# Gated cross-attention and experts block: another order of work inside a slot, and half of the weights' low parts on another engine

## The reference, cut to what matters

```python
x = x + tanh(g_xattn) * xattn(layernorm(x), ctx)      # 16 heads of 8, softmax, Wout
x = x + tanh(g_ffn)   * ffn(layernorm(x))
# ffn, x [8, 128, 128]:
gate = softmax(x @ Wg.T); topk_val, topk_idx = top_k(gate, 2)
comb = (one_hot(topk_idx) * (topk_val / (sum(topk_val) + 1e-9))[..., None]).sum(-2)
for e in range(8):
    a, b = split(x @ W1[e].T + b1[e], 2)               # 256 + 256
    out += ((a * sigmoid(b)) @ Wo.T + bo) * comb[..., e]
```

## Time and profile before

| | |
|---|---|
| median of 3 runs | 126.2 us (124.78, 126.2, 126.21) |
| the profiled execution, own time | 124.31 us |
| its span | 122.2 us |
| busy: PE, DVE, ACT, POOL | 111.3, 99.6, 66.1, 83.7 us |
| weights loading (PEld) | 76.7 us |
| granted TensorE clock over the span | 0.998 of full speed |

### The profile page before, as it was taken

The page is one execution under the profiler, slowest core; times in us unless marked ns, Lnnn a source line. Parts: engine busy times, 40 slices in busy tenths (PEclk is TensorE's granted clock), DMA queues, the critical chain, the costliest instruction groups (busy, mean ns, idle before and its releaser), DMA issues.

```text
span 122.2 us, 2512 instructions
## 1 busy us (share of the span) xinstructions
PE 111.3 (91%) x808; PEld 76.7 (63%) x810; DVE 99.6 (81%) x274; ACT 66.1 (54%) x145; POOL 83.7 (68%) x106
## 2 busy tenths in 40 slices
PE   6989798899699979797979999999999799999982
PEld 2254554466466646564746877878686687878661
DVE  5489999779897989898795969599999778776770
ACT  3166467849586866675768266543433334343520
POOL 6359879997989599984235587857273987574600
PEclk9999999999999999999999999999999999999999
DMA  3999970000000000000000000000000000000001
GB/s 92 325 360 414 421 303 5 0 0 8 0 3 0 0 8 0 0 5 0 0 0 0 0 5 3 0 21 0 21 5 3 21 20 2 0 24 0 21 0 43
DMA packets 3468, 6.53 MB, mean 53 GB/s; under 512 B 384, under 2 KB 2048, under 8 KB 3456
## 3 DMA queue, kind: packets, MB, share of 16 engines
q1 hardware_dynamic: 3024, 5.66, 12.8%
q10 hardware_dynamic: 432, 0.72, 1.7%
HBM read 5.85 MB, written 0.52 MB: 52 GB/s over the span
## 4 chain that ended last, share of the span: by engine, by line
PE 52%; DVE 29%; issue 11%; ACT 4%; POOL 2%; DVEq 0%; ACTq 0%; POOLq 0%
PE ps L955 11%; PE ps L957 10%; PE ps L956 10%; DVE neg_max L613 9%; DVE gl L685 3%; PE ps L974 2%; PE ps L927 2%; DVE qk_lo L600 2%; PE ps L904 2%; DVE w_lo L796 2%; DVE max_m L792 2%; PE ps L1094 2%; ACT sig L448 1%; PE ps L984 1%; DVE att L783 1%
## 5 line engine op out<-in xcount | busy, mean ns | idle before, releaser
L328 POOL TENSOR_TENSOR gacc<-gacc,gl 128x256 f32<-128x256 f32 x38 | 28.6, 753 | 12.9 <-DVE gl L685 9.4
L448 ACT ACTIVATE sig<-ps 128x512 f32<-128x512 f32 (+1 forms) x33 | 19.3, 585 | 28.3 <-PE ps L957 25.8
L685 DVE SCALAR_TENSOR_TENSOR gl<-ps,comb,sig 128x256 f32<-128x256 f32 (+1 forms) x57 | 24.6, 471 | 5.0 <-ACT sig L448 4.7
L955 PE MATMUL ps<-w_hi,x_hi 128*128 128x512 f32 x64 | 27.3, 427 | 0.0
L956 PE MATMUL ps<-w_lo,x_hi 128*128 128x512 f32 x64 | 25.3, 395 | 0.0
L957 PE MATMUL ps<-w_hi,x_lo 128*128 128x512 f32 x64 | 25.3, 395 | 0.0
L394 ACT ACTIVATE probs<-ps 128x1024 f32<-128x1024 f32 x16 | 16.4, 1024 | 7.7 <-PE ps L914 7.5
L613 DVE TENSOR_REDUCE neg_max<-ps 128x8 f32<-128x1024 f32 x16 | 19.4, 1215 | 0.7 <-PE ps L887 0.6
L955 PEld LDWEIGHTS ps<-w_hi,x_hi 128*128 128x128 f32 x64 | 12.1, 188 | 3.0 <-DVE gl L685 0.6
L957 PEld LDWEIGHTS ps<-w_hi,x_lo 128*128 128x128 f32 x64 | 12.0, 188 | 2.9
L956 PEld LDWEIGHTS ps<-w_lo,x_hi 128*128 128x128 f32 x64 | 12.1, 190 | 1.9
(11 more groups left out here) (126 smaller groups left out, 209.4 us busy)
## 6 DMA issues: line engine op xcount, KB each, us to landing
...
```

The costliest lines, as they stand in the source:

```text
L328: nc.gpsimd.tensor_tensor(gacc[:, t % 2, :], gacc[:, t % 2, :], gl[:, e - 1, :], ALU.add).then_inc(pool_experts_added, 1)
L448: nc.scalar.activation(sig[:, n % 3, e[0]:e[1], :], ps[:, b + e[0]:b + e[1], HH:H2], ACT.Sigmoid).then_inc(act_sigmoids, 1)
L685: nc.vector.scalar_tensor_tensor(dst[:, c[0]:c[1]], ps[:, 2 * (n % 3) + e % 2, c[0]:c[1]], comb[:, t, e:e + 1], sig[:, n % 3, e % 2, c[0]: ...
L955: mm(o, x_hi[:, t, :], w_hi[:, e, :], start=True, stop=False)
```

## The change

It leaves nearly all instructions as they are and places them otherwise in the slots:

- **PE.** `weighted(i-1, 1)` now stands behind the first scores of the slot, ahead of the values' projection and of Wout. The turn of `o_sb` stands ahead of the second scores, and the turn of `att` right behind them. In odd slots the turn of `xn2` moves behind the first scores. The idle matmuls of slot 1 are dropped.
- **DVE.** `rden` and `att` go between the instructions of the moments and ahead of the second maxima. `low_parts` moves to the end of even slots. The bias for the values (`bvl`) is made after the second maxima of slot 0 and not ahead of `max_m`, and `bout_t` is made in slot 1.
- **ACT.** `values_out` goes ahead of `values_in`.
- **POOL.** In even slots it makes `w_lo` of expert i, at the end of its slot, once ACT has rounded `w_hi`. DVE makes those of the odd slots alone.

The diff, cut to its core:

```diff
+                if on(i) and i % 2 == 0:
+                    pool.wait_ge(act_w1_high, i + 1)
+                    nc.gpsimd.tensor_tensor(w_lo[:, i, :], w1[:, i, :], w_hi[:, i, :].bitcast(fp32),
+                                            ALU.subtract).then_inc(pool_w1_low, 1)
...
-                if i % 2 == 1 and i != 1 and on(i + 3):
+                if i in (-3, -1):
                     xn_turned_out((i + 3) // 2)
                 if on(i):
                     exp(i, 0)
-                if i == 1:
-                    xn_turned_out(2)
+                if i % 2 == 1 and i >= 1 and on(i + 3):
+                    xn_turned_out((i + 3) // 2)
                 if i == 0:
                     high_parts(1)
+                if on(i - 1) and i < T:
+                    values_out(i - 1)
                 if i % 2 == 0 and on(i + 2):
                     values_in((i + 2) // 2)
-                if on(i - 1) and i < T:
-                    values_out(i - 1)
...
+                    "p k (h c) -> p k h c", h=2)
+
+            rd = rden[:, :].rearrange("p (k h) -> p k h", h=2)
+            sums_inverted = [0]
...
+            def inverse_sums(t):
+                dve.wait_ge(pe_values_turned, t + 1)
+                sums_inverted[0] = mark(nc.vector.reciprocal(rd, attended_heads()[:, :, :, HD]))
+
+            def attended(t):
+                if t >= 2:
+                    dve.wait_ge(pe_attended_turned, t - 1)
+                dve.wait_ge(dve_chain, sums_inverted[0])
+                nc.vector.tensor_tensor(att[:, t % 2, :].rearrange("p (k h c) -> p k h c", h=2, c=HD),
...
-                if on(i - 3):
-                    t = i - 3
-                    dve.wait_ge(act_xn2, 2 * (t + 1))
...
+                if on(i - 3) and (i % 2 == 0 or i >= T):
+                    x_low(i - 3)
                 if on(i + 1):
                     maxima(i + 1, 0)
+                if on(i - 3) and i % 2 == 1 and i < T:
+                    x_low(i - 3)
                 if i == 0:
-                    statistics(2)
-                if i % 2 == 0 and i > 0 and on(i + 2):
-                    low_parts((i + 2) // 2)
+                    late = moments(2)
+                if i == 1:
+                    dve.wait_ge(pe_value_bias, 1)
+                    nc.vector.scalar_tensor_tensor(bout_t[:, :], boutb, tanh_g[:, 0:1], ps[:, VEB, 0:D], ALU.mult,
+                                                   ALU.add).then_inc(dve_bout_scaled, 1)
                 if on(i - 2):
...
-                    link(nc.vector.bn_stats(stats2[:, t % 2, :], x1[:, t, :]))
-                    link(nc.vector.bn_aggr(mv2[:, t % 2, :], stats2[:, t % 2, :]))
+                    moments2 = mark(nc.vector.bn_stats(stats2[:, t % 2, :], x1[:, t, :]))
+                if on(i - 1) and i < T:
+                    inverse_sums(i - 1)
+                if on(i - 2):
+                    t = i - 2
+                    dve.wait_ge(dve_chain, moments2)
+                    moments2 = mark(nc.vector.bn_aggr(mv2[:, t % 2, :], stats2[:, t % 2, :]))
+                if on(i - 1) and i < T:
+                    attended(i - 1)
+                if on(i - 2):
+                    t = i - 2
+                    dve.wait_ge(dve_chain, moments2)
                     nc.vector.tensor_scalar(var2[:, t % 2:t % 2 + 1], mv2[:, t % 2, 1:2], LN_EPS, None,
                                             ALU.add).then_inc(dve_variance2, 1)
...
                 if i == 0:
-                    low_parts(1)
-                if i == -1:
-                    low_parts(0, (1,))
+                    variances(2, late)
                     dve.wait_ge(dve_ones, 1)
                     nc.vector.tensor_scalar(bvl[:, :], ones_r[:, :].bitcast(fp32), bvc, None,
                                             ALU.mult).then_inc(dve_v_bias, 1)
+                    nc.vector.tensor_tensor(wgT[:, :], wg_in, wg_last, ALU.subtract).then_inc(dve_ffn_weights, 1)
...
-                if i == 0:
...
-                    nc.vector.tensor_tensor(wgT[:, :], wg_in, wg_last, ALU.subtract).then_inc(dve_ffn_weights, 1)
...
-                if on(i - 1):
-                    t = i - 1
-                    dve.wait_ge(pe_values_turned, t + 1)
...
-                        dve.wait_ge(pe_attended_turned, t - 1)
-                    link(nc.vector.reciprocal(rd, o[:, :, :, HD]))
-                    nc.vector.tensor_tensor(att[:, t % 2, :].rearrange("p (k h c) -> p k h c", h=2, c=HD),
...
+                if i == T:
+                    inverse_sums(T - 1)
+                    attended(T - 1)
...
-                if on(i):
+                if i % 2 == 0 and i >= 0 and on(i + 2):
+                    low_parts((i + 2) // 2)
+                if on(i) and i % 2 == 1:
                     dve.wait_ge(act_w1_high, i + 1)
                     nc.vector.tensor_tensor(w_lo[:, i, :], w1[:, i, :], w_hi[:, i, :].bitcast(fp32),
                                             ALU.subtract).then_inc(dve_w1_low, 1)
...
+            def turn_values(t):
+                pe.wait_ge(act_values, t + 1)
+                if t == 0:
+                    pe.wait_ge(dve_bout_scaled, 1)
+                else:
+                    pe.wait_ge(dve_x1, t)
...
+            def turn_attended(t):
+                pe.wait_ge(dve_attended, t + 1)
+                pe.wait_ge(act_v, min((t + 1) // 2 + 2, NP))
+                if t >= 2:
+                    pe.wait_ge(act_logits, t - 1)
+                nc.tensor.transpose(ps[:, AB, 0:P], att[:, t % 2, :], ident).then_inc(pe_attended_turned, 1)
...
+            def turn_xn2(t):
+                i = t + 3
+                if i <= T + 1:
+                    pe.wait_ge(act_attended, i - 1)
+                else:
+                    pe.wait_ge(act_gated, 1)
+                pe.wait_ge(act_normed2, t + 1)
+                nc.tensor.transpose(ps[:, AB, 0:P], xn2[:, t % 2, :], ident).then_inc(pe_xn2_turned, 1)
...
-                    pe.wait_ge(dve_w1_low, 2 * j + 2)
+                    pe.wait_ge(pool_w1_low, j + 1)
+                    pe.wait_ge(dve_w1_low, j + 1)
...
-                if i % 2 == 1 and i != 1 and on(i + 3):
-                    turn_xn((i + 3) // 2)
-                if on(i - 3):
...
                 if i == -1:
+                    turn_xn(1)
                     keep_busy(FILL[3], PVB)
+                if i == -3:
+                    turn_xn(0)
+                if on(i - 3) and (i % 2 == 0 or i >= T):
+                    turn_xn2(i - 3)
                 if on(i):
                     scores(i, 0)
                 if i == 0:
                     project(1)
-                if i == 1:
-                    turn_xn(2)
+                if i % 2 == 1 and 3 <= i < T:
+                    turn_xn2(i - 3)
+                if i % 2 == 1 and i >= 1 and on(i + 3):
+                    turn_xn((i + 3) // 2)
+                if on(i - 1) and i < T:
+                    weighted(i - 1, 1)
                 if i % 2 == 0 and on(i + 2):
                     project_values((i + 2) // 2)
                 if on(i - 2):
...
-                if on(i - 1) and i < T:
-                    weighted(i - 1, 1)
+                if i == 1:
+                    pe.wait_ge(act_out_weights, 1)
+                    pe.wait_ge(dve_v_bias, 1)
+                    pe.wait_ge(dve_max_masked, 2)
+                    mm(ps[:, VEB, 0:D], bvl[:, :], wout_t[:, :], start=True, stop=True).then_inc(pe_value_bias, 1)
...
+                if on(i - 1) and i < T:
+                    turn_values(i - 1)
                 if on(i):
                     scores(i, 1)
-                if i == 0:
...
-                    mm(ps[:, VEB, 0:D], bvl[:, :], wout_t[:, :], start=True, stop=True).then_inc(pe_value_bias, 1)
-                if on(i - 1):
-                    t = i - 1
-                    pe.wait_ge(act_values, t + 1)
-                    if t == 0:
-                        pe.wait_ge(dve_max_masked, 2)
-                    else:
-                        pe.wait_ge(dve_x1, t)
...
+                if on(i - 1) and i < T:
+                    turn_attended(i - 1)
+                if i == T:
+                    turn_values(T - 1)
                 if on(i):
                     weighted(i, 0)
-                if on(i):
-                    pe.wait_ge(act_v, min(i // 2 + 2, NP))
-                    if i >= 3:
-                        pe.wait_ge(act_logits, i - 2)
-                    keep_busy(WARM[0] if i < 2 else WARM[1], AB)
+                if i == 0:
+                    pe.wait_ge(act_v, 2)
+                    keep_busy(WARM, AB)
...
-                    if t == 1:
-                        pe.wait_ge(dve_bout_scaled, 1)
-                    elif t >= 2:
+                    if t >= 2:
                         pe.wait_ge(dve_attended, t - 1)
                     nc.tensor.transpose(ps[:, VEB, 0:P], neg_max[:, t % 2, :], ident).then_inc(pe_maxima_turned, 1)
-                if on(i - 1):
-                    t = i - 1
```

(34 more changed lines are left out.)

45 lines of the change are left out of this document (13 added, 32 removed).

## The result

The changed kernel is slower: 138.6 us median of four executions (133.72, 142.42, 134.86, 142.59) against 125.5 us (124.03 to 126.21). The ratio is 1.080 [1.055, 1.104]. Each ratio in this document is made from a kernel's executions within about 1.5% of its fastest, so it leaves out most of those whose clock fell, while a median holds them all. What sets the four apart is the clock of TensorE: their spans are 131.9, 140.6, 133.1 and 140.8 us at a mean granted clock of 0.934, 0.842, 0.897 and 0.842. My forecast was 127.6 us, with a range from 124.0 to 130.3. What follows is read from the execution of 133.72 us, against the profiled 124.31 us of before (span 122.2).

A forecast was written before the change was run, and what follows sets the result against it. It took the succession of slots 0 to 7 as the bound, with POOL late after the change. Start +1.4, slots 4 and 5 +1.26, slot 6 -0.5, slot 7 -0.7, rounded to +1.4 on 126.2: 127.6 us, range 124.0 to 130.3.

The forecast's parts named there:

- the sum: 1.4 + 1.26 - 0.5 - 0.7 = +1.5 us, rounded down to +1.4, over the start, slots 4 and 5, 6, and 7.
- Part 1: Turn of the maxima on PE no longer behind `att`: gain of 0.6 us per slot, hidden because POOL is late.
- Part 2: `rden`, `att` before the second maxima: S (start of a slot's first score matmul) to `var` 4.23 us, even slots.
- Part 3: Half of `w_lo` moved to POOL: POOL pays 1.27 us each, `q_lo_m` in even slots 1.0, DVE regains 0.68 to 0.84.
- rival of a stretched POOL: POOL's `w_lo` and weights run at 1.72 us, `q_lo_m` at 1.49, as beside DVE's `w_lo`: 130.3 us; chance 0.20.
- Part 4: Chain from `var` through POOL, ACT and PE, slots 4 and 5: 13.67 us a pair against 12.41, +1.26.
- Part 5: Start: up to 1.9 us earlier, but POOL's first `w_lo` waits for `w_hi`; S(4) at 40.2, +1.4 us.
- Part 6: Slot 6, without projection, -0.5 us; slot 7, with `att` made ahead of the routing, -0.7 us.
- Part 7: Edits at nothing: `values_out` ahead of `values_in`, `wgT`, `bout_t`, turn of `xn2` behind the first scores in odd slots.
- fit in: Rival: POOL has room, slot pairs cost what they did, the rest is gain, -2.8 us: 123.4 us; chance 0.15.
- even out: Rival: two unknown handovers at 0.33, slots 4 and 5 cost nothing, S(4) 0.5 late: -0.7, 125.5 us; chance 0.20.
- chance of slower: Probability of a time above 128.7 us, 0.29: 0.18 from stretched POOL, 0.11 from the forecast's own case.

The follow-up runs named there:

- experiment 9: The changed kernel plus idle matmuls wherever its PE was seen to wait (slots 1 to 3 and 5 to 7): 128.3 us, ratio 1.027.
- experiment 11: The changed kernel with only POOL's first `w_lo` moved from slot 0 to slot 6: 124.75, 133.66, 127.42 and 133.12 us.
- experiment 8: The kernel before, with DVE's `rden` and `att` of slot 7 ahead of the routing: 125.4 us, ratio 1.007.
- number 10: The changed kernel with POOL's four `w_lo` moved to slots 6 and 7, plus six idle matmuls in slot 1: 124.7 us, ratio 1.002.
- Number 3: The changed kernel with four idle matmuls behind each turn of the maxima in slots 1 to 6: 131.4 us, ratio 1.053.

## Why the prediction was wrong

**The step that failed** is one that the sum did not have: it took PE's clock as 1.00 throughout. The last sentence of the prediction called a lower granted clock "a cost that the sum lacks". I read 1.00 in both stretches and went on, with no rival and no bound for it. It measured 6.2 us of the 9.7 (experiment 9), and more in the executions of 142 us. The danger could have been seen: the change adds waits to PE in a stage where PE already stood idle 0.89 of 10 us, and takes idle matmuls away in the same place. What the trace of before could not give is how many gaps are too many: from 30 to 32 us its PE worked 1.18 of 2 us, and its clock stayed at 1.00. Nor do the runs give it as a rule: in one and the same kernel (11) the clock held once and fell three times.

The queues were priced too low besides. With the clock held (experiment 9) they cost 3.5 us, where the sum had 1.5:

| | S(4) | S(4) to S(6) | slot 6 | S(7) to the end |
|---|---|---|---|---|
| foreseen | +1.4 | +1.26 | -0.5 | -0.7 |
| with the clock held | +2.6 | +0.9 | -0.6 | +0.6 |

By its own parts:

- **Part 1, right.** The turn of the maxima waits for nothing (54.90 above), where the earlier trace rows had 0.28 for `att`. As the prediction said, the gain does not show.
- **Part 2, right.** S to `var` was put at 4.23 us in even slots. With the clock held (experiment 9) it is 45.63 - 41.41 = 4.22 in slot 4, and no term is off by more than 0.12. Of the two handovers that no row showed, Wout (begun at 43.66) to `x1` took 0.42, where I took 0.54, and the turns (begun at 44.60) to `rden` 0.46, where I took 0.50. DVE waits 0.67 and 0.36 for them:

```profile
44.08 0.29 DVE L789 TENSOR_TENSOR x<-ps,x 128x128 f32<-128x128 f32 x1 [0.67 <-PE ps L1112]
45.06 0.26 DVE L733 RECIPROCAL rden<-ps 128x16 f32<-128x16 f32 x1 [0.36 <-PE ps L888]
...
45.63 0.14 DVE L803 TENSOR_SCALAR var<-mv 128x1 f32<-128x1 f32 x1
```

- **Part 3, right.** POOL's four `w_lo` take 1.28 us in the mean, and `q_lo_m` fell from 1.32 to 1.09. The price was read off the right row: `w` has a median of 1.27 both before and after. The lines of POOL after:

```profile
L322 POOL TENSOR_TENSOR w<-w,w1l 128x512 f32<-128x512 f32 x8 | 10.6, 1328 | 0.0
L317 POOL TENSOR_TENSOR q_lo_m<-qk_lo,pk 128x512 fp32r<-128x512 f32 x8 | 8.8, 1094 | 0.0
...
L367 POOL TENSOR_TENSOR w_lo<-w,w_hi 128x512 fp32r<-128x512 f32 x4 | 5.1, 1276 | 1.5 <-ACT w_hi L522 1.5
```

  The rival of a stretched POOL falls with this: none of the four ran at 1.72. Beside one of them (experiment 9, begun at 47.72) DVE ran both `qk_lo`, at 47.93 and 48.33, and it took 1.29 us, as the prediction expected of operands in PSUM. POOL was stretched in other places, though: its sum `x` took 2.83 us, not 2.37, beside DVE's `w_lo` of slot 1 (at 25.25), and one of the eight `w` took 1.73.
- **Part 4, right in its mechanism, somewhat high in size.** From S(4) to S(6) I put 13.67 us. It is 13.54 after, in part at a lower clock, and 13.31 with the clock held: +0.9 to +1.1 against +1.26. By its terms, with the clock held: S to `var` 4.22; from `var` to the end of the weights (50.96 + 1.28) 6.61, where I had 6.63; from there to S(6), at 54.72, 2.48, where I had 2.81. The last term is the one that is off. It also left out 0.24 us that the earlier trace rows show, ACT's wait ahead of `attT`: those rows give 51.20 - 48.15 = 3.05. In the new order `att` is turned early and that wait is gone, but I gave no such reason.
- **Part 5, right in its mechanism, short in size.** `w_lo` of slot 0 begins at 20.07 behind ACT (19.8 foreseen), `w_hi` of slot 3 at 37.98 (37.4 foreseen). S(4) was put at 40.2 and came at 42.18. Of these 2.0 us, 0.5 is POOL (the weights end at 37.94; nearly all of it is the stretched `x`). The other 1.4 lie between the weights and S(4), 4.24 us and not 2.81. With the clock held and no matmul added, the same piece takes 2.90 us (experiment 11: 36.01 to 38.91), so 1.3 of it is the clock. That 2.90 lies near my 2.81 is in part luck, as the path is another one. In the chain of the kernel after it doesn't go through `xn2` and `attT`: the turn of `att` on PE waits for `lg`, the copied logits, which come behind ACT's late `w_hi` (0.42 in the row at 38.81, and 0.44 in experiment 11), and PE's own work follows it up to S(4). POOL's delay reaches PE through more than one reader of ACT's queue. In experiment 9, S(4) is 1.2 us later than foreseen: 1.0 up to the end of the weights (38.38, not 37.4), 0.2 from there.
- **Part 6, half right.** Slot 6 took 60.04 - 54.72 = 5.32 us with the clock held, 5.36 foreseen. Slot 7's 0.7 is not there; experiment 8 shows that the routing pays for it. In experiment 9 `comb` begins 8.3 us after S(7) (68.33 - 60.04), not 5.8, and from S(7) to the end it takes 0.6 us more than before, not less.
- **Part 7**, the edits put at nothing: no run tests them one by one. The sign "expert stage of the same length" failed: from S(7) to the end it took 68.0 us, not 65.1, as the first matmuls ran at half speed up to 70 us; with the clock held it is 65.7.

**The rivals.** POOL does not fit in, nor does it even out: `w_hi` of slot 3 began at 37.98, not before 36. The chance of slower, 0.29, was too small because its cases priced only queues. Had the clock been a rival, rows of before could have bounded its price. As an estimate: ten us like those of the earlier trace rows hold 9.11 us of PE's work, which at half the clock would fill 18.2 us, so a long fall in this stage costs several us.

**What stays open** is why the clock falls at 21 us in one kernel, at 39 and 56 in another, and not at all in another execution of the same. Gaps of PE come ahead of each fall in the traces, but the same traces also have gaps without one. That filling the gaps holds the clock is shown by experiment 9 (four executions of four, where the change fell in all four, and number 11 in three of four in the same comparison as number 9), and number 10 agrees. Number 3 suggests that the idle matmuls must stand where PE waits. How much is enough was not settled.
